# A graph-attention layer whose fp32 score products are split in halves, its mask moved to GpSimd, its statistics combined a slot later, and its input kept in eight buffers

## The reference

```python
Q = x @ q;  K = x @ k
A = einsum('bnd,bmd->bnm', Q, K) / sqrt(128)
A = exp(tanh(A / 8) * 8) * adj
A = A / sum(A, axis=-1, keepdims=True)
x = layernorm(x + A @ x @ v)
```

## Time and profile before

| | |
|---|---|
| median of 3 runs | 1387.19 us (1386.95 to 1387.49) |
| the profiled execution | 1387.39 us, of which its span is 1385.2 |
| attention | about 6 to 190 us of the span |
| busy | PE 97%, DVE 80%, ACT 67%, POOL 54% |
| granted TensorE clock | 0.992 over the span |

### The profile page before, as it was taken

One profiled execution on the slowest core, in us unless ns is written; L12 is line 12 of the kernel. 1 busy time (PEld: TensorE's weight loads), 2 busy tenths in 40 slices (PEclk: granted clock), 3 DMA queues, 4 the chain that ended last, 5 costly groups with the idle time before them and its releaser, 6 DMA issues.

```text
span 1385.2 us, 26908 instructions
## 1 busy us (share of the span) xinstructions
PE 1349.8 (97%) x8470; PEld 1184.3 (85%) x8470; DVE 1108.6 (80%) x2632; ACT 927.9 (67%) x1666; POOL 753.7 (54%) x745
## 2 busy tenths in 40 slices
PE   9999979999999999999999999999889999999995
PEld 7888868888888888888888888887689999999994
DVE  5888878777778777778777787777688888888885
ACT  5666647677777776777777777766546666666664
POOL 4111127666666666666666666665435555555553
PEclk9999999999999999999999999999999999999998
DMA  3222232000021000020000110000212222222211
GB/s 107 96 92 91 96 103 77 1 0 0 9 82 32 0 0 0 30 83 8 0 0 0 46 46 1 0 0 8 76 54 70 70 68 68 68 68 68 68 39 38
DMA packets 60041, 61.16 MB, mean 44 GB/s; under 512 B 4691, under 2 KB 39381, under 8 KB 59989
## 3 DMA queue, kind: packets, MB, share of 16 engines
q1 hardware_dynamic: 59556, 60.31, 13.6%
q10 hardware_dynamic: 432, 0.20, 0.1%
HBM read 35.33 MB, written 25.17 MB: 44 GB/s over the span
## 4 chain that ended last, share of the span: by engine, by line
PE 94%; DVE 3%; ACT 2%; issue 1%; POOL 0%; ACTq 0%; POOLq 0%; DVEq 0%
PE psum L969 6%; PE psum L663 5%; PE psum L665 5%; PE psum L651 5%; PE psum L346 4%; PE psum L365 4%; PE psum L981 3%; PE psum L983 3%; PE psum L706 3%; PE psum L695 3%; PE psum L678 3%; PE psum L707 3%; PE psum L676 3%; PE psum L696 3%; PE psum L699 3%; PE psum L698 3%
## 5 line engine op out<-in xcount | busy, mean ns | idle before, releaser
L626 POOL TENSOR_TENSOR rh_lo<-rh,rh_hi 128x512 fp32r<-128x512 f32 x160 | 207.1, 1294 | 265.6 <-ACT rh_hi L741 265.6
L632 POOL TENSOR_TENSOR h_lo<-h,h_hi 128x512 fp32r<-128x512 f32 x160 | 216.6, 1354 | 12.8
L741 ACT CAST rh_hi<-rh 128x512 fp32r<-128x512 f32 x160 | 99.4, 621 | 149.2 <-DVE rh L773 149.2
L754 DVE TENSOR_TENSOR psum<-psum,h 128x512 f32<-128x512 f32 x160 | 111.9, 699 | 103.5 <-ACT psum L745 103.5
L663 PE MATMUL psum<-adj_t_hi,hn_hi 128*128 128x256 f32 x640 | 172.1, 303 | 1.0 <-DVE m_lo L767 1.0
L738 ACT ACTIVATE psum<-psum,bias_cols 128x512 f32<-128x512 f32 x160 | 106.8, 667 | 80.1 <-PE psum L683 80.0
L665 PE MATMUL psum<-adj_t_hi,hn_lo 128*128 128x256 f32 x640 | 158.9, 282 | 0.0
L773 DVE TENSOR_TENSOR rh<-psum,h 128x512 f32<-128x512 f32 x160 | 110.1, 688 | 50.3 <-ACT psum L738 50.2
L663 PEld LDWEIGHTS psum<-adj_t_hi,hn_hi 128*128 128x128 f32 x640 | 121.8, 190 | 1.9 <-issue 1.8
L665 PEld LDWEIGHTS psum<-adj_t_hi,hn_lo 128*128 128x128 f32 x640 | 122.2, 191 | 0.0
L728 ACT ACTIVATE z<-psum,bias_cols 128x512 f32<-128x512 f32 x160 | 111.3, 695 | 0.0
(11 more groups left out here) (184 smaller groups left out, 4119.8 us busy)
## 6 DMA issues: line engine op xcount, KB each, us to landing
x_in<-in_x_dram SPq DMA_DIRECT2D x32, 256.0 KB, 2.8
x_dram<-x SPq DMA_DIRECT2D x32, 256.0 KB, 2.1
g_x<-x_dram SPq DMA_DIRECT2D x32, 256.0 KB, 3.3
h_dram<-h SPq DMA_DIRECT2D x32, 256.0 KB, 2.0
ht<-h_dram SPq DMA_DIRECT2D x32, 256.0 KB, 2.9
c_x<-x_dram SPq DMA_DIRECT2D x32, 256.0 KB, 3.1
out_dram<-res SPq DMA_DIRECT2D x32, 256.0 KB, 2.4
conv_in<-in_L_gnn_weight_dram SPq DMA_DIRECT2D x1, 448.0 KB, 4.8
```

Of the source, the lines that this page charges most:

```text
L626: pool.tensor_tensor(rh_lo[:, q, :], rh[:, q, :], rh_hi[:, q, :].bitcast(F32), ALU.subtract).then_inc(rh_lo_done, 1)
L632: pool.tensor_tensor(h_lo[:, q, :], h[:, (g - 1) % G, :], h_hi[:, q, :].bitcast(F32), ALU.subtract).then_inc(h_lo_done, 1)
L754: dve.tensor_tensor(cb, cb, hg, ALU.subtract).then_inc(dif_done, 1)
```

## The change

- **Split halves in S and P.** `x_t` is cut into `xt_hi` (GpSimd) and `xt_lo` (VectorE, from PSUM), P into `p_hi` (ScalarE) and `p_lo` (VectorE, from PSUM), qk into `qk_hi` and `qk_lo`. S becomes twelve fp32r products of 256 columns, P three of 512.
- **TensorE's order** in a slot becomes XT(s), O(s-3), S(s-1), XV(s), P(s). P waits for `xt_lo` of its own group.
- **The mask** moves from VectorE to GpSimd, same shape, behind `xt_hi` and in front of the power.
- **Combining** moves from the end of slot s (group s-3) to near the start of the next one (group s-4), behind `p_lo`. Normalising is for group s-5; half of it stays on VectorE, the other half goes to ScalarE as two activations of 128x128, which need `shift` = -mean * rstd, a new small product on GpSimd. The store of `x1` waits for both halves and comes a slot later.
- **x** has eight buffers, and the loop is unrolled eight times; `e`, `xv` and `y` have four.
- **GpSimd's preparation** of weights moves from in front of its loop to between the slots 0 to 6; TensorE's and VectorE's share of it stands behind slot 1. GpSimd first waits for `x_t` of the slot and only then does `shift` and `xt_hi`.

```diff
-    U = 4
-    LAG_S, LAG_MASK, LAG_OUT, LAG_NORM, LAG_STORE = 1, 2, 3, 4, 5
-    PEELED = 2
+    U, R = 8, 4
+    LAG_S, LAG_MASK, LAG_OUT, LAG_COMBINE, LAG_NORM, LAG_STORE = 1, 2, 3, 4, 5, 6
+    PEELED = 1
...
+                sp.wait_ge(x1_half_done, n + 1)
...
         def slot(it, u):
-            n, q = it * U + u, u % 2
-
-            pool.wait_ge(var_done, n + 1)
-            pool.tensor_tensor(rstd[:, q, :], var_eps[:, q, :], minus_half[:, :], ALU.pow).then_inc(rstd_done, 1)
-        yield from run(pool, slot, 0, behind=LAG_OUT)
+            s = it * U + u
+            if live(it, u, 0):
+                pool.wait_ge(xt_done, s + 1)
+                wait_count(pool, s_mm, s - 1)
+            if live(it, u, LAG_NORM):
+                n, q = s - LAG_NORM, (u - LAG_NORM) % 2
+                pool.wait_ge(rstd_done, n + 1)
+                wait_count(pool, x1_half_done, n - 1)
+                pool.tensor_tensor(shift[:, q, :], mv[:, q, :, 1], rstd[:, q, :], ALU.mult).then_inc(shift_done, 1)
+            if live(it, u, 0):
+                pool.tensor_copy(xt_hi[:, u % 2, :], x_t[:, u % 2, :]).then_inc(xt_hi_done, 1)
+            if live(it, u, LAG_MASK):
...
+                pool.wait_ge(exp_done, n + 1)
...
+                pool.tensor_tensor(eb, eb, mask, ALU.mult).then_inc(e_done, 1)
+            if live(it, u, LAG_COMBINE):
+                n, q = s - LAG_COMBINE, (u - LAG_COMBINE) % 2
+                pool.wait_ge(var_done, n + 1)
...
+                pool.tensor_tensor(rstd[:, q, :], var_eps[:, q, :], minus_half[:, :], ALU.pow).then_inc(rstd_done, 1)
+        yield from run(pool, slot, LAG_NORM, prepare)
...
+                        pe.matmul(dst, xt_hi[:, q, tile], p_hi[:, q, cols], start=True, stop=False)
+                        pe.matmul(dst, xt_lo[:, q, tile], p_hi[:, q, cols], start=False, stop=False)
+                        mm = pe.matmul(dst, xt_hi[:, q, tile], p_lo[:, q, cols], start=False, stop=True)
...
+                pe.wait_ge(xt_lo_done, s + 1)
...
+                pe.matmul(psum[:, B_P, :], qk_hi[:, :], xt_hi[:, u % 2, :], start=True, stop=False)
+                pe.matmul(psum[:, B_P, :], qk_lo[:, :], xt_hi[:, u % 2, :], start=False, stop=False)
+                pe.matmul(psum[:, B_P, :], qk_hi[:, :], xt_lo[:, u % 2, :], start=False, stop=True).then_inc(p_mm, 1)
```

ScalarE's order in a slot becomes `p_hi`(s-1), `x_t`(s), exp(s-2), half of `x1`(s-5), tanh(s-1), `xv`(s). VectorE's function:

```diff
         def slot(it, u):
+            if live(it, u, LAG_S):
...
+                dve.tensor_tensor(p_lo[:, q, :], psum[:, B_P, :], p_hi[:, q, :].bitcast(F32),
+                                  ALU.subtract).then_inc(p_lo_done, 1)
+            if live(it, u, LAG_COMBINE):
...
+                combine_stats(dve, stats[:, q, :, :], mv[:, q, :, :], parts[:, q, :, :], var_eps[:, q, :],
+                              parts_done, mv_done, var_done, n)
             if live(it, u, LAG_OUT):
...
+            if live(it, u, 0):
+                dve.wait_ge(xt_hi_done, s + 1)
+                wait_count(dve, s_mm, s - 1)
+                dve.tensor_tensor(xt_lo[:, u % 2, :], psum[:, B_XT, :], xt_hi[:, u % 2, :].bitcast(F32),
+                                  ALU.subtract).then_inc(xt_lo_done, 1)
+            if live(it, u, LAG_OUT):
                 dve.wait_ge(y_done, n + 1)
```

More of the change, by code:

```diff
@@ L102, in _ @@
                 def _(pool):
-                    both = weave(attention["gpsimd"](pool), gated["gpsimd"](pool), [30, 31, 32, 33])
+                    both = weave(attention["gpsimd"](pool), gated["gpsimd"](pool), [31, 32, 33, 34])
                     for _ in weave(both, conv["gpsimd"](pool), [155, 159, 162]):
@@ L164, in attention_layer @@
     x_t = sb("x_t", [128, 2, COLS])
-    p_t = sb("p_t", [128, 2, COLS])
-    xv = sb("xv", [128, U, TILES, 132])
+    xt_hi = sb("xt_hi", [128, 2, COLS], F32R)
+    xt_lo = sb("xt_lo", [128, 2, COLS], F32R)
+    p_hi = sb("p_hi", [128, 2, COLS], F32R)
+    p_lo = sb("p_lo", [128, 2, COLS], F32R)
+    qk_hi = sb("qk_hi", [128, D], F32R)
+    qk_lo = sb("qk_lo", [128, D], F32R)
+    shift = sb("shift", [128, 2, TILES])
+    HALF = TILES // 2
+    xv = sb("xv", [128, R, TILES, 132])
     cap = sb("cap", [128, 2 * COLS])
-    e = sb("e", [128, U, TILES, N])
-    y = sb("y", [128, 2, TILES, D])
+    e = sb("e", [128, R, TILES, N])
+    y = sb("y", [128, R, TILES, D])
     x1 = sb("x1", [128, 2, TILES, D])
@@ L215, in attention_layer, with run @@
     B_QKT, B_QK, B_ADJ, B_U, B_W = 4, 5, 6, 7, 2
[L217 to L225, removed]
+    def run(eng, slot, lags, between=None, second=None):
+        for s in range(PEELED * U):
+            slot(s // U, s % U)
+            if second is not None:
+                second(s // U, s % U)
+            if between is not None:
+                between(s)
         with eng.Fori(PEELED, GROUPS // U - 1) as it:
@@ L233, in run @@
             if second is not None:
-                yield s + behind - 0.5
+                yield s - 0.5
                 second(s // U, s % U)
-            yield s + behind
+            yield s
     def live(it, u, lag):
@@ L297, in gpsimd @@
[L297 to L304, removed]
@@ L334, in slot @@
             s = it * U + u
+            if live(it, u, 0):
+                pe.wait_ge(x_loaded[u], (it + 1) * 16)
+                wait_count(pe, xt_lo_done, s)
+                for i in range(TILES):
+                    mm = pe.transpose(psum[:, B_XT, i * 128:(i + 1) * 128], x_in[:, u, i, :], ident[:, :])
+                mm.then_inc(xt_mm, 1)
             if live(it, u, LAG_OUT):
-                n, r = s - LAG_OUT, (u - LAG_OUT) % U
+                n, r = s - LAG_OUT, (u - LAG_OUT) % R
                 pe.wait_ge(e_done, n + 1)
@@ L349, in slot @@
                 mm.then_inc(o_mm, 1)
[L350 to L356, removed]
             if live(it, u, LAG_S):
                 n, q = s - LAG_S, (u - LAG_S) % 2
-                pe.wait_ge(pt_done, n + 1)
+                pe.wait_ge(p_lo_done, n + 1)
                 wait_count(pe, cap_done, n)
@@ L364, in slot @@
                         i = b * KC + k
[L365 to L366 removed]
+                        dst = psum[:, B_S + b, k * N:(k + 1) * N]
+                        tile, cols = slice(i * 128, (i + 1) * 128), slice(b * N, (b + 1) * N)
+                        pe.matmul(dst, xt_hi[:, q, tile], p_hi[:, q, cols], start=True, stop=False)
+                        pe.matmul(dst, xt_lo[:, q, tile], p_hi[:, q, cols], start=False, stop=False)
+                        mm = pe.matmul(dst, xt_hi[:, q, tile], p_lo[:, q, cols], start=False, stop=True)
                 mm.then_inc(s_mm, 1)
@@ L370, in slot @@
                 pe.wait_ge(xt_done, s + 1)
[L371 to L374, removed]
                 wait_count(pe, xv_done, s)
@@ L382, in slot, with weights @@
                 mm.then_inc(xv_mm, 1)
-        def weights():
+                pe.wait_ge(xt_lo_done, s + 1)
+                if isinstance(it, int) and s == 0:
+                    pe.wait_ge(qk_done, 1)
+                pe.matmul(psum[:, B_P, :], qk_hi[:, :], xt_hi[:, u % 2, :], start=True, stop=False)
+                pe.matmul(psum[:, B_P, :], qk_lo[:, :], xt_hi[:, u % 2, :], start=False, stop=False)
+                pe.matmul(psum[:, B_P, :], qk_hi[:, :], xt_lo[:, u % 2, :], start=False, stop=True).then_inc(p_mm, 1)
+        def weights(s):
+            if s != 1:
+                return
             pe.wait_ge(w_ready, 1)
@@ L412, in slot @@
             s = it * U + u
+            if live(it, u, LAG_S):
+                n, q = s - LAG_S, (u - LAG_S) % 2
+                act.wait_ge(p_mm, n + 1)
+                wait_count(act, s_mm, n - 1)
+                act.copy(p_hi[:, q, :], psum[:, B_P, :]).then_inc(p_hi_done, 1)
             if live(it, u, 0):
                 act.wait_ge(xt_mm, s + 1)
-                wait_count(act, s_mm, s - 1)
                 wait_count(act, xv_mm, s - 1)
                 act.copy(x_t[:, u % 2, :], psum[:, B_XT, :]).then_inc(xt_done, 1)
+            if live(it, u, LAG_MASK):
+                n, r = s - LAG_MASK, (u - LAG_MASK) % R
+                act.wait_ge(cap_done, n + 1)
+                wait_count(act, o_mm, n - R + 1)
+                act.activation(e[:, r, :, :].rearrange("p i n -> p (i n)"), cap[:, :], ACT.Exp,
+                               scale=8.0).then_inc(exp_done, 1)
+            if live(it, u, LAG_NORM):
+                n, q = s - LAG_NORM, (u - LAG_NORM) % 2
+                act.wait_ge(shift_done, n + 1)
+                if not isinstance(it, int):
+                    act.wait_ge(x1_out[q], it * (16 * U // 2) + 16 * ((u - LAG_NORM) // 2))
+                elif n >= 2:
+                    act.wait_ge(x1_out[q], 16 * (n // 2))
+                for i in range(HALF, TILES):
+                    op = act.activation(x1[:, q, i, :], y[:, (u - LAG_NORM) % R, i, :], ACT.Identity,
+                                        bias=shift[:, q, i:i + 1], scale=rstd[:, q, i:i + 1])
+                op.then_inc(x1_half_done, 1)
             if live(it, u, LAG_S):
-                n, r = s - LAG_S, (u - LAG_S) % U
```

(3 more changed lines are left out.)

157 lines of the change are left out of this document (89 added, 68 removed).

## The result

The changed kernel takes 1443.33 us (median of 5 runs, 1438.41 to 1446.37) against 1387.26 us (5 runs, 1386.95 to 1387.96): a ratio of 1.041, 95% interval 1.038 to 1.043. It is slower by 56 us; 1382.3 was forecast, and the time lies far outside 1373 to 1392. The profiled execution, the shortest of the five, took 1438.41 us with a span of 1436.6, which is 51.4 more than before's 1385.2.

The account below looks back on a forecast made before the run. TensorE's order was taken as the bound, 32 attention slots of 5.71 us. Steady slots -9.4, start +0.5 and hand-over +4 gave -4.9: 1387.2 to 1382.3 us, range 1373 to 1392.

Parts of the forecast that it names:

- Two engines that hold each other up: Step on VectorE instructions waiting for GpSimd's: in steady slots L140 gets in before the mask, loss 0 to 0.1 us.
- The first rival: Combining loses the port to GpSimd in each attention slot: slot 7.5 us, +49, 1436 us; chance 0.10.
- TensorE's pieces: TensorE's work in an attention slot: 0.44 + 1.79 + 1.36 + 0.90 + 0.69 = 5.18 us, 0.53 less.
- The chain: In an attention slot P waits for `xt_lo`, which stands behind `y`: P starts at 4.64, slot 5.33, taken as 5.30.
- Start: Attention slots 0 to 8, with GpSimd's preparation between masks and possible collisions in slots 4 and 6: +0.5 us.
- steady part: Attention slots 9 to 31, 23 slots: 23 x (5.71 - 5.30) = 9.4 us less.
- hand-over: Where attention passes to the gated layer: +1 (no collision) to +9 us, taken as +4.
- the sum of -4.9: Whole-kernel change: -9.4 (slots 9 to 31) + 0.5 (slots 0 to 8) + 4 (passing to the gated layer) us.
- The buffers: Eight buffers for x in attention: cost and gain nothing by themselves, but without them the slot would be about 6.6 us.

Follow-up runs that it names:

- The fastest version: Changed kernel with combining ahead of `p_lo`, and GpSimd's `shift` and `xt_hi` also waiting for L140: 1379.83 us, ratio to before 0.995.

## Why the prediction was wrong, point by point

**The step that failed** stands under "Two engines that hold each other up": after `x_t` ends near 1.25, "GpSimd passes three more waits, does shift, and starts xt_hi near 1.85, after L136". Measured from XT at 100.54: `x_t` over at 1.27, `p_lo` at 0.81 and L132 at 1.42 are as forecast (1.25, 0.8, 1.4). But `shift` starts 0.07 behind the end of `x_t`, so three waits whose semaphores are already there cost nothing that can be seen, and `xt_hi` starts at 1.48. It meets L133 in place of following L136. The mask, too, is a little early, 2.30 and not 2.5. What the forecast put at a loss of "0 to 0.1" is 2.1 in a slot. The kernel with the mask behind L140 shows this to be the cause: only the collision of L140 with the mask is removed, and the whole loss comes back. The half mask shows the mechanism, since 1.1 us less of GpSimd's instruction are 1.1 us less of slot. Two slots of the changed kernel itself go as the forecast had it: in slots 17 and 25 `xt_hi` starts 1.90 behind XT, L140 ends with it, 0.2 before the mask starts, and the slots take 6.76 and 6.41. TensorE's transposes ran at 1.2 GHz there (1.05 in place of 0.60) and made `x_t`, and so `xt_hi`, late; the slot came out shorter at the slower clock.

The first rival had the numbers: a slot of 7.5 (measured 7.45), 1436 (profiled 1438.41, though the median is 7 us higher), by the very condition "if GpSimd's waits are cheaper than I think by 0.1"; `xt_hi` was 0.37 early. Its path differed in one link: the hold on L133, not on L136, carried L140 behind the mask. What was wrong was its chance of 0.10. The forecast itself said that 0.1 us decides between +0 and +49, and the 0.3 us for the waits was no row of the trace; a coin toss would have been the fair weight. The Trainium skill, "SBUF — State Buffer", Terms, which says that the loser of the shared port pair fully blocks for the whole instruction, is borne out by the 2.23 beside 2.41. It is not borne out by the power, inside which nothing was held (last section).

**TensorE's pieces.** Forecast 5.18, measured 5.24 when nothing else holds it. The two new terms were a little short, S 1.51 for 1.36 and P 0.78 for 0.69, and O (1.70 for 1.79) and XV (0.81 for 0.90) were put too long: +0.24 and -0.18. That the sum is off by only 0.06 is luck, for the two errors have nothing to do with each other. The gain of the split is 0.46 for 0.53.

**The chain** `y`, `xt_lo`, P: forecast 5.33 with P at 4.64 behind XT, taken 5.30; with combining still behind `p_lo` the slot is 5.38 and P starts at 4.59, with it in front 5.24. Right, and with combining first TensorE is the bound and not the chain.

**GpSimd.** The mask was taken at 2.4 and takes 2.40; it was said to be hidden, and is, even 0.46 later. VectorE's and ScalarE's new work fills neither.

**Start, steady part and hand-over**, without the collision. In the kernel where the mask waits, XT of slot 9 comes 0.4 later than before (forecast 0.5), the 22 slots up to XT of slot 31 save 7.1 (9.0 by 5.30 a slot), and the sixth transposes of the gated layer come 4.0 later (forecast 4). That is -2.7; its span is 4.6 shorter. The fastest version has +1.6, -10.0 and +3.3, which is -5.1, with a span 7.3 shorter. Its +1.6 is one stretch at 1.2 GHz (19.1 to 22.5 us, after TensorE had worked 1.4 of 3.5 us): slot 2 takes 7.37 there and 5.80 in the kernel where the mask waits. So the sum of -4.9 describes the change without its collision rather well, in part by luck: it holds two collisions at the start that these kernels do not have in slots 4 and 6. The 2 us that the later layers gain beyond that are not explained.

In the changed kernel the start loses 9.0, not 0.5: slots 0 to 3 take 3.6 to 5.8, and as soon as combining begins, in slot 4, a slot is 6.2 to 8.1. The forecast had the collision in slots 4 and 6 alone. The second transposes of the gated layer come 17.0 behind the last XT, where 10 to 15 were forecast (9.3 before; 12.2 and 11.6 in the two kernels above). In all the hand-over loses 9.3, the top of its +1 to +9. The clock is not the cause: 7.7 of the 9.3 are lost up to those second transposes, where the granted clock is 1.00 (225 to 242 us), and behind them the kernel before has two stretches at 1.2 GHz and the changed one a single one. Held operations stand there instead, L140 2.23 at 228.12, L138 2.38 at 236.35, `hn_lo` 1.46 at 241.00; how the 9.3 divide among them was not taken apart.

**The buffers.** "Without them the slot would be about 6.6": measured 6.8 on average, and 38 us. With eight, XT waits 0.2 us once in the fastest version between 60 and 165 us.

## What to carry to other kernels

Before moving an elementwise operation to GpSimd, list each small VectorE operation on SBUF that can start inside it and what stands behind that on VectorE; a 2.4 us GpSimd instruction lends its whole length to a 0.16 us one. Where the order of two engines is decided by 0.1 or 0.2 us, don't reckon it out: fix it, by placing the small operations where GpSimd is idle, or by one wait in front of the long instruction, which here left the mask hidden and was worth 60 us. When a move costs time in one place, test the parts together before judging them: here taking back the split, the move of the mask or the eight buffers costs 12, 26 and 38 us, each in a kernel that is only 2 to 3 us faster than the one before.

## What the hardware showed that was not expected

Operations with a single SBUF input are held too. In a slot of the changed kernel in which GpSimd came a little later, L135 and L138 met the hold:

```profile
117.26 0.61 POOL L353 CAST xt_hi<-x_t 128x512 fp32r<-128x512 f32 x1
117.29 0.61 DVE L135 TENSOR_SCALAR parts<-mv 128x4 f32<-128x4 f32 x1
...
117.83 2.38 POOL L362 TENSOR_TENSOR e<-e,adj_t 128x1024 f32<-128x1024 f32 x1
117.88 2.36 DVE L138 TENSOR_SCALAR mv<-mv 128x4 f32<-128x4 f32 x1
```

The forecast counted only the four operations with two SBUF inputs. Operations that read PSUM are not held: in the fastest version reciprocal, `y` and `xt_lo` run inside the mask, and keep their 0.18, 1.13 and 0.68:

```profile
142.20 2.39 POOL L364 TENSOR_TENSOR e<-e,adj_t 128x1024 f32<-128x1024 f32 x1
142.31 0.18 DVE L524 RECIPROCAL den<-psum 128x4 f32<-128x4 f32 x1 [0.49 <-PE psum L394]
142.53 1.13 DVE L527 SCALAR_TENSOR_TENSOR y<-psum,den,x_in 128x128 f32<-128x128 f32 x4
143.57 0.68 DVE L533 TENSOR_TENSOR xt_lo<-psum,xt_hi 128x512 fp32r<-128x512 f32 x1
```

Statistics (one SBUF input, 128x128) are not held either: in the hand-over of the kernel before, four start inside `h_lo` (193.36, 1.26) from 193.88 on and take 0.28 to 0.30 each, as elsewhere.

It depends on GpSimd's instruction, too. In the fastest version nothing that VectorE starts inside the power is held, be it normalising (144.95 inside 144.55 to 145.58, 0.59 for two) or the small operations of the combining, with one SBUF input or two:

```profile
50.06 1.07 POOL L370 TENSOR_TENSOR rstd<-var_eps,minus_half 128x4 f32<-128x4 f32 x1
50.63 0.17 DVE L132 TENSOR_TENSOR mv<-stats 128x12 f32<-128x12 f32 x1
...
50.91 0.17 DVE L135 TENSOR_SCALAR parts<-mv 128x4 f32<-128x4 f32 x1
```

Normalising itself can be held. In the hand-over of the changed kernel its second operation starts 0.11 behind `h_lo`, and the two take 1.57 in place of 0.59:

```profile
250.87 1.57 DVE L549 TENSOR_SCALAR x<-y,mv,rstd 128x128 f32<-128x128 f32 x2
251.01 1.35 POOL L709 TENSOR_TENSOR h_lo<-h,h_hi 128x512 fp32r<-128x512 f32 x1
```

Why the power holds nobody, these runs do not show.

Being held does not always end with the first GpSimd instruction. L133 got in between `xt_hi` and the mask, which were 0.21 apart, while L135 in the kernel with combining in front stood 3.56 us behind four GpSimd instructions that followed each other without a gap. The missing gap does not decide it alone: at 117.83 the mask follows `xt_hi` without one, and L135 still ends there.

TensorE's granted clock is 0.96 between 60 and 140 us of the changed kernel, where it idles 1.6 us a slot before P: full clock, with single stretches of 3.4 us at 1.2 GHz. It is 1.00 in the fastest version, and also with slots of 6.8 in the kernel with four buffers.

The five runs of the changed kernel spread over 8 us, against 1 us for the five of the kernel before beside it (and 5 us for later ones). Its shortest run has a mean granted clock of 0.988, the other four 0.978 to 0.982. L140 wins or loses by 0.2 us, so either may be the reason, and no run was made to tell them apart.
